# ODE stage of a four-layer hybrid network: sums left in PSUM, tanh read from there twice, the low part by a scan, 48 matmuls of four columns

## The reference

```
f(y) = tanh(tanh(y W1' + b1) W2' + b2) W3' + b3        (W1: 512x128, W2: 512x512, W3: 128x512)
k1 = f(y); k2 = f(y + dt/2 k1); k3 = f(y + dt/2 k2); k4 = f(y + dt k3)
y  = y + dt (k1 + 2 k2 + 2 k3 + k4) / 6
```

## Time and profile before

| what | value |
|---|---|
| median of 3 runs | 8713.31 us (8688.4 to 8720.65) |
| the profiled execution: its own time, its span | 8689.44 us, 8687.6 us |
| mean granted TensorE clock | 0.929 |
| PE matmul busy | 8034.5 us (92%) |
| PE weight loads busy | 5075.3 us (58%) |
| DVE busy | 5725.2 us (66%) |
| ACT busy | 2697.7 us (31%) |
| POOL busy | 1221.5 us (14%) |
| L803, the real matmuls of the products | 3940.5 us in 130816 |
| L815, `keep_busy` | 3260.8 us in 12264 |
| first and last matmul of the products start at | 899.9 and 7459.1 us |

### The profile page before, as it was taken

The page is one execution under the profiler, slowest core; times in us unless marked ns, Lnnn a source line. Parts: engine busy times, 40 slices in busy tenths (PEclk is TensorE's granted clock), DMA queues, the critical chain, the costliest instruction groups (busy, mean ns, idle before and its releaser), DMA issues. The chain is left out here.

```text
span 8687.6 us, 384742 instructions
## 1 busy us (share of the span) xinstructions
PE 8034.5 (92%) x148469; PEld 5075.3 (58%) x148469; DVE 5725.2 (66%) x32782; ACT 2697.7 (31%) x10082; POOL 1221.5 (14%) x5222
## 2 busy tenths in 40 slices
PE   8994899999999999999999999999999999765886
PEld 3221566666666666666666666666666666444765
DVE  4334666666666666666666666666666666546997
ACT  2221222222222222222222222222222222235886
POOL 1000111111111111111111111111111111001001
PEclk7665999999999999999999999999999999767887
DMA  1000000100010000100010001000000000002332
GB/s 43 1 0 32 15 4 4 38 4 4 4 38 4 4 4 4 38 4 4 4 38 4 4 4 38 4 4 4 8 34 4 4 4 20 3 0 109 121 126 75
DMA packets 44973, 185.48 MB, mean 21 GB/s; under 512 B 7156, under 2 KB 27319, under 8 KB 33031
## 3 DMA queue, kind: packets, MB, share of 16 engines
q1 hardware_dynamic: 38662, 145.18, 4.4%
q0 software_dynamic: 4480, 15.38, 0.5%
HBM read 122.93 MB, written 37.62 MB: 18 GB/s over the span
## 5 line engine op out<-in xcount | busy, mean ns | idle before, releaser
L803 PEld LDWEIGHTS p<-H,W 128*128 128x128 f16 x130816 | 3571.6, 96 | 1931.7 <-DVE H L954 1914.2
L803 PE MATMUL p<-H,W 128*128 128x8 f16 x130816 | 3940.5, 167 | 66.1 <-DVE H L954 59.1
L815 PE MATMUL p<-W 128*128 128x500 f16 x12264 | 3260.8, 374 | 0.0
L954 DVE SCALAR_TENSOR_TENSOR H<-h,H 128x8 f16<-128x8 f32 x10220 | 1505.7, 164 | 282.0 <-DVE H L949 2.6
L889 ACT ACTIVATE h<-u 128x8 f32<-128x8 f32 x4088 | 852.2, 208 | 2428.2 <-DVE u L980 2269.3
L884 ACT ACTIVATE h<-r 128x8 f32<-128x8 f32 x4088 | 851.6, 208 | 2404.6 <-DVE r L988 2217.7
L988 DVE TENSOR_REDUCE r<-p 128x8 f32<-128x24 f32 x4088 | 746.1, 183 | 1050.9 <-PE p L803 809.9
L980 DVE TENSOR_REDUCE u<-p 128x8 f32<-128x24 f32 x6132 | 964.9, 175 | 717.8 <-PE p L803 716.9
L949 DVE TENSOR_SCALAR H<-h 128x8 f16<-128x8 f32 x8176 | 1400.1, 171 | 40.8 <-ACT h L884 21.7
L815 PEld LDWEIGHTS p<-W 128*128 128x128 f16 x12264 | 886.0, 96 | 473.4 <-issue 9.3
L779 POOL TENSOR_TENSOR twice<-r 128x16 f32<-128x16 f32 x511 | 110.2, 216 | 2860.1 <-DVE r L988 2860.1
(11 more groups left out here) (364 smaller groups left out, 4211.5 us busy)
## 6 DMA issues: line engine op xcount, KB each, us to landing
e_W<-w_scaled SPq DMA_DIRECT2D x23, 2304.0 KB
e_W<-w_scaled SPq DMA_DIRECT2D x23, 1152.0 KB, 5.2
raw_f<-in_spline SPq DMA_DIRECT2D x21, 1024.0 KB, 6.3
w_scaled<-raw_f SPq DMA_DIRECT2D x7, 2304.0 KB, 7.6
w_scaled<-raw_f SPq DMA_DIRECT2D x7, 1152.0 KB, 11.2
raw<-in_spline POOLq DMA_DIRECT2D x3, 1024.0 KB, 6.8
rows_in<-zeros POOLq DMA_DIRECT2D x4, 768.0 KB, 12.5
e_xs<-rows_in SPq DMA_DIRECT2D x12, 256.0 KB, 5.6
```

The source lines that it names most:

```text
L803: ins = pe.matmul(out[:, m, 0:2 * B], W[:, q, k, P * m:P * m + P], H[:, k, :, :].rearrange("p q b -> p (q b)"), start=fresh[m], stop=(left ...
L815: pe.matmul(out[:, k, 3 * B:S], W2[:, 0, k, 0:P], W2[:, 1, k, 3 * B:S], start=True, stop=True, skip_group_check=True)
L954: sg.up(dve.scalar_tensor_tensor(out=Hq[:, :, 1, :], in0=mb(cols(h, q)), scalar=HSCALE, in1=Hq[:, :, 0, :], op0=ALU.mult, op1=ALU.subtract ...
```

## The change

- `keep_busy`, the scale of 4096 on H, the reductions (L980, L988), `high` and `low` go.
- The sums stay in PSUM. Every product adds on top of a seed that DVE writes into columns 0 to 3 of each bank beforehand (`start=False` everywhere; eight matmuls with zeros before the loop). The first product on `p2` is seeded with b2, by a copy of `b2s`; `p1` is seeded with the Runge-Kutta terms.
- ACT takes tanh straight from PSUM, twice: once into H (fp16) and once into h (fp32).
- The output chunks go in three groups, (0), (1, 2) and (3), in both layers: six ACT instructions to a product.
- H, h and L hold three slots for each value; constants in slots 1 and 2 make one DVE scan along the line leave 4096 (h - H) in slot 1 of L.
- The low part is multiplied by the high weight part alone, scaled down by 4096 (`W2D`, `W13D`). A block is then two matmuls with H and one with L: 48 matmuls of 4 columns, in the order of one list BLOCKS for both layers, where "h" stands for two matmuls and "l" for one.
- DVE copies `p1` into r once the tanh has been taken, and POOL works from that copy.

```
-    FILL = 3
-    RED2, LOW2 = [(0, 1), (2,), (3,)], [(0, 1), (2,), (3,)]
...
+    GROUPS = [(0,), (1, 2), (3,)]
+    G = len(GROUPS)
+    LIFT = 4096.0
+    BLOCKS = [("h", 0, 2), ("h", 0, 3), ("h", 0, 0), ("h", 0, 1), ("h", 2, 0), ("h", 2, 2), ("h", 2, 1), ("h", 1, 0), ("l", 0, 2),
+              ("h", 3, 1), ("h", 3, 2), ("l", 1, 2), ("l", 1, 0), ("l", 0, 0), ("l", 2, 1), ("l", 0, 3), ("l", 1, 1), ("l", 2, 0),
+              ("h", 3, 0), ("l", 3, 0), ("h", 1, 1), ("l", 3, 2), ("l", 2, 2), ("h", 1, 2), ("l", 3, 1), ("l", 0, 1), ("h", 3, 3),
+              ("l", 2, 3), ("h", 1, 3), ("l", 3, 3), ("l", 1, 3), ("h", 2, 3)]
...
+        H1, H2 = sb("H1", [P, NV, 3], F16), sb("H2", [P, NV, 3], F16)
+        h1, h2 = sb("h1", [P, NV, 3]), sb("h2", [P, 4, NV, 3])
+        L1, L2 = sb("L1", [P, NV, 3], F16), sb("L2", [P, NV, 3], F16)
...
+        def product(pe, i, w, e, out, W, WD, H, L, high, low, seeded, n_seeded, done):
+
+            wait(pe, seeded, n_seeded, w, i)
+            left, owed, high_in, low_in = [2 * KH] * KH, list(GROUPS), 0, 0
+            for part, k, m in BLOCKS:
+                group = next(n for n, q in enumerate(GROUPS) if k in q) + 1
+                if part == "h" and group > high_in:
+                    wait(pe, high, 2 * (G * e + group) - 1, w, i)
+                    high_in = group
+                if part == "l" and group > low_in:
+                    wait(pe, low, G * e + group, w, i)
+                    low_in = group
...
+                columns = slice(B * k, B * k + B)
+                terms = [(W[:, q, k, P * m:P * m + P], H[:, columns, 0]) for q in range(NP)] if part == "h" else [
+                    (WD[:, k, P * m:P * m + P], L[:, columns, 1])]
+                for n, (weights, x) in enumerate(terms):
+                    ins = pe.matmul(out[:, m, 0:B], weights, x, start=False, stop=(left[m] == 0 and n == len(terms) - 1), skip_group_check=True)
...
-        def keep_busy(pe, out):
-
-
-            for k in range(FILL):
-                pe.matmul(out[:, k, 3 * B:S], W2[:, 0, k, 0:P], W2[:, 1, k, 3 * B:S], start=True, stop=True, skip_group_check=True)
...
+                        product(pe, i, w, e, p2, W2, W2D, H1, L1, "h1", "lo1", "seed2", e + 1, "u2")
+                        product(pe, i, w, e, p1, W13, W13D, H2, L2, "h2", "lo2", "seed1", e + 1, "u1")
...
+            for n, (wd, whole) in enumerate(((W2D, W2), (W13D, W13))):
+                sg.wait(act, "part", n + 1)
+                sg.up(act.activation(wd[:], whole[:, 0], ACT.Copy, scale=1.0 / LIFT), "part")
...
+                            for n, q in enumerate(GROUPS):
+                                wait(act, "u1", G * e + n + 1, w, i)
+                                for x in (H1, h1):
+                                    sg.up(act.activation(mb(cols(x[:, :, 0], q)), sums(p1[:, q[0]:q[-1] + 1]), ACT.Tanh, scale=factor[c]), "h1")
...
+            def low(H, h, L, layer, e, n, w, i):
+                wait(dve, f"h{layer}", 2 * (G * e + n + 1), w, i)
+                sg.up(dve.tensor_tensor_scan(flat(cols(L, GROUPS[n])), flat(cols(H, GROUPS[n])), flat(cols(h, GROUPS[n])), -1.0, ALU.mult, ALU.add), f"lo{layer}")
...
+                        for n in range(G):
+                            low(H1, h1, L1, 1, e, n, w, i)
+                        before = r[:, (e + 3) % 4, :]
+                        sg.up(dve.tensor_copy(mb(before), sums(p1)), "copied")
+                        wait(dve, "copied", e + 1, w, i)
...
+                        for n in range(G):
+                            low(H2, h2[:, e], L2, 2, e, n, w, i)
+                        sg.up(dve.tensor_copy(sums(p2), mb(b2s[:])), "seed2")
```

More of the change, by code:

```diff
@@ L745, in flow @@
         mb = lambda x: x.rearrange("p (m b) -> p m b", b=B)
-        terms = lambda x, q: x[:, q[0]:q[-1] + 1, 0:3 * B].rearrange("p m (q b) -> p m b q", b=B)
-        seed = lambda x: x[:, :, 2 * B:3 * B]
+        flat = lambda x: x.rearrange("p n s -> p (n s)")
+        sums = lambda x: x[:, :, 0:B]
         splits = [(w2f[:], lambda q: W2[:, q]), (w13f[:], lambda q: W13[:, q])]
@@ L769, in _ @@
             sg.up(pool.memset(hist[:, :, STEPS:S, :], 0.0), "ones_set")
+            sg.up(pool.memset(zero[:], 0.0), "zeros")
+            for x in (H1, H2):
+                sg.up(pool.memset(x[:, :, 1], LIFT), "zeros")
+                sg.up(pool.memset(x[:, :, 2], 0.0), "zeros")
+            sg.up(pool.memset(h1[:, :, 1], 0.0), "zeros")
+            sg.up(pool.memset(h1[:, :, 2], -1.0), "zeros")
+            for e in range(4):
+                sg.up(pool.memset(h2[:, e, :, 1], 0.0), "zeros")
+                sg.up(pool.memset(h2[:, e, :, 2], -1.0), "zeros")
             sg.wait(pool, "ones_set", 3)
@@ L781, in _ @@
                     sg.up(pool.tensor_tensor(base[:], twice[:], third[:], ALU.add), "base")
[L783 to L786, removed]
+                    wait(pool, "h2", 6 * G, w, i)
+                    sg.seq(pool, pool.tensor_tensor(inner[:], h2[:, 1, :, 0], h2[:, 2, :, 0], ALU.add), "hsum", i)
+                    wait(pool, "h2", 8 * G, w, i)
+                    sg.seq(pool, pool.tensor_tensor(outer[:], h2[:, 0, :, 0], h2[:, 3, :, 0], ALU.add), "hsum", i)
                     sg.seq(pool, pool.tensor_tensor(both[:], inner[:], outer[:], ALU.add), "hsum", i)
@@ L837, in _ @@
             sg.wait(pe, "rest", 2)
+            sg.wait(pe, "zeros", 1)
+            for x in (p1, p2):
+                for m in range(KH):
+                    ins = pe.matmul(x[:, m, 0:B], W2[:, 0, m, 0:P], zero[:], start=True, stop=True)
+                sg.up(ins, "cleared")
             with pe.Fori(0, STEPS // UN) as i:
@@ L959, in _ @@
                     for e in range(4):
-                        at1, at2 = len(HIGH1) * e, len(HIGH2) * e
-                        high(h1, H1, 1, (0, 1), at1 + 1, w, i)
-                        low(h1, H1, 1, (0, 1), at1 + 1, w, i)
-                        high(h1, H1, 1, (2, 3), at1 + 2, w, i)
-                        low(h1, H1, 1, (2, 3), at1 + 2, w, i)
+                        for n in range(G):
[3 more added lines that the diff above has]
+                        wait(dve, "copied", e + 1, w, i)
+                        if e < 3:
+                            seed = dve.scalar_tensor_tensor(out=sums(p1), in0=mb(r[:, 3, :]), scalar=(1.0 / 3.0, 1.0 / 3.0, 1.0 / 6.0)[e], in1=mb(hb[:]), op0=ALU.mult, op1=ALU.add)
+                        else:
+                            wait(dve, "base", 6, w, i)
+                            seed = dve.scalar_tensor_tensor(out=sums(p1), in0=mb(r[:, 2, :]), scalar=2.0, in1=mb(base[:]), op0=ALU.mult, op1=ALU.add)
+                        sg.up(seed, "seed1")
                         if e == 1 and 4 <= w < 4 + 2 * ExpertWeights.PARTS:
```

99 lines of the change are left out of this document (24 added, 75 removed).

## The result

The changed kernel takes 8748.31 us (median of 20 runs, 8709.89 to 8759.08); the kernel before took 8712.25 beside it (20 runs, 8677.12 to 8734.51). The ratio is 1.0035, 95% interval 1.0022 to 1.0048. I had predicted 7485 in a range of 7270 to 8200, so the time lies outside the range: no gain, a small loss. It is rival C in mechanism, to which I had given 0.07 and a time of 8,620.

The account below looks back on a forecast made before the run. It took the round trip PE, DVE, ACT (1.583 us a product) as the bound, then PE's own work: 2216.9 us plus 4087 x 1.282 = 5239.5 gives a span of 7456, carried over to 7482, given as 7485; range 7270 to 8200.

Parts of the forecast that it names:

- rival C: PE in the ODE waits for its instruction packets; a product takes 1.4 to 1.56 us, up to 8,620 us; chance 0.07.
- the time table: One product step by step: every input reaches PE in time by 0.03 to 0.14 us, so PE's 1.282 us binds.
- The 1.07 us: Time an instruction packet itself takes in the DMA engines, held against waiting for instructions.
- the 3.7 us of the turn: PE's standstill at each of six loop turns, 22 us in all; also taken as a possible time per instruction packet.
- break-even: Product time in the ODE at which the change gains nothing: 1.583 us.
- The clock: PE without filler runs at 1.2 GHz (0.50) through the ODE, 3 in 4; 26.7 ns a pair, 1.282 us a product.
- D: PE can't keep its pace beyond a burst; slower than before from 33 ns a pair, at most 11,110 us; chance 0.11.
- ACT and DVE: Per product, six tanh of 183 ns, starting 0.11 us apart, and DVE scans of 185 and 210 ns.
- B: The round trip by ACT and DVE clearly binds each product; 7,720 to 8,300 us; chance 0.22.
- The rest of the sum: Outside the products: 899.9 + 3.7 ahead, 81 for turns and hiccups, 1229.3 + 3 behind; 2216.9 us.
- The two copies: Two more ACT copies of 1.91 us in set-up before the loop, adding 3.7 us.
- my formula: Whole kernel time T = 2242.6 + 4087 p, for a product of p us.

Follow-up runs that it names:

- pe_loop_7: Changed kernel with PE's loop rolled up to seven evaluations (14 products, some 1400 instructions) as its body: 7547.14 us, 0.8701 of the kernel before.
- low_twice_loop: Changed kernel with each of the 16 low-part matmuls of a product issued twice and PE looping over one evaluation: 9361.79 us.
- pe_loop_1: Changed kernel with PE's loop rolled up to one evaluation (2 products, some 200 instructions) as its body: 7753.09 us, 0.8923 of the kernel before.
- pe_loop_14: Changed kernel with PE's loop over 14 evaluations (28 products, some 2800 instructions) as its body: 9384.56 us.
- two_groups: Changed kernel, still unrolled, with output chunks in two groups, (0, 1) and (2, 3), instead of three, and BLOCKS to fit: 8469.70 us, 0.973 of the changed kernel.
- act_pool_loop: Changed kernel, PE unrolled, with only ACT's and POOL's loops rolled up to one Runge-Kutta step: 8683.04 us, 0.9984 of the kernel before.
- one_filler: Changed kernel with one unread matmul of 508 columns added to each product to raise the clock: 9328.39 us.
- no_low: Changed kernel with the 16 low-part matmuls of a product left out of PE's work, scans still running: 6837.18 us.

## Why the prediction was wrong

**The step that failed** is the conclusion of the time table, "So PE's own work becomes the bound", which took instructions to be always at hand, together with the weight of rival C: "packets themselves take 1.07 us [...], and PE's rows show next to no 'issue'. 0.07". What stood in its place: PE waited for its instructions, one packet in 4.10 us, so that a product took 1.616 us and not 1.282. The numbers of C were all there: 7.0 KB a product (measured 6.46), a packet used up in 3.0 us (the products at hand use one in 1.28 / 0.394 = 3.2), 3.7 us for a packet if it is as slow as at the turn (4.10). What I did wrong was to hold two rows against it that say nothing of it. The 1.07 us is what a packet's bytes take in the DMA engines; between two packets of PE's queue lie 3.8 to 4.1 us in the kernels kept waiting, while that queue fills 1.7 to 1.9% of the DMA engines. And the absence of "issue" in the kernel before only said that 5.6 us is enough. A rate that has never been asked for is not shown by a trace in which nobody waits for it. The nearest row was the 3.7 us of the turn, and it should have carried the sum; its own label names DVE, not "issue", which is why it can give C a price but no proof.

**C's size.** With 3.7 us it gave p = 1.56 and 8,620; measured are 4.10 and 8,748. There is a slip in it: 7.0 / 16.4 x 3.7 is 1.58 us, and 8,700, which is break-even. My range ended at 8,200, and I had counted C among the gains, while by its own numbers nothing was left to gain.

**The clock: right.** 0.50 through the ODE; between stalls and in pe_loop_7 a product takes 1.28 or 1.33 us where I had 1.282 from 26.7 ns a pair. That the pace of pairs holds beyond a burst (D) is shown by low_twice_loop.

**ACT and DVE: right.** Scans 183 and 208 ns for 185 and 210; tanh 181, 171 and 190 for 183; the distance of two tanh 0.07 for 0.11, better than I had. The row that I had read the 0.11 from the earlier trace rows gives 0.10, and the other one 0.08 by my 0.183. The round trip (B) didn't bind: the waits for ACT and DVE in the changed kernel are at most 28 of 1000 us, those of pe_loop_7 2.8. Why every second product takes 1.33 and not 1.28 I haven't found; the list BLOCKS is the same for both, so it isn't the list.

**The rest of the sum.** Ahead of the first product 7.8 us were added, not 3.7. The two copies take the 3.7 (they follow the last split of the weights from 902.47 and end ahead of the table load for tanh at 906.18); nearly all the rest lies ahead of that split, which starts at 900.66 instead of 896.03. The traces differ there anyway: the first product starts between 871.5 us (pe_loop_1) and 924.4 (pe_loop_14), and at 872.0 in two_groups, which is unrolled. Behind the last lie 8750.2 - 7518.5 = 1231.7 us; I had 1229.3 + 3. None of it matters. If I put the p of pe_loop_7 into my formula, 2242.6 + 4087 x 1.328 = 7,670, it lies 120 above the 7547 measured. The main reason is that a p counted over 1000 us has the turns and hiccups in it already, and the formula adds 81 us for them: for the kernel before, the p of 1.603 overshoots by 80 us in the same way. The first product of pe_loop_7 also starts 24 us earlier (879.3) than the formula has it, and its profiled execution lies only 2 below the median, not 24.

**So where did the gain go?** The chain through ACT and DVE did become short enough for PE's own work to be the bound, and the rolled-up kernels show what that is worth: 13% in pe_loop_7. In the unrolled one it went into PE's wait for instructions, 0.394 of a packet a product. The kernel before hid 0.29 of a packet (180 over 623.7 products) behind a chain of 1.58 us; the change took the cover away and asked for 37% more at once.

**The Trainium skill on this.** "Runtime: NRT & Kernel Launch", section "Instruction fetch mechanics", says that instructions come in blocks of 256, that PE holds 2048, that fetching them is hidden because issuing is slower than the fill, and that a taken branch outside a window of two blocks stalls. The runs agree on the block (64 bytes, 16.4 KB), and on the capacity as far as they go: 1400 stay, 2800 don't. They disagree with the fill being hidden (244 to 263 blocks in 1000 us, PE standing in between), and with the window of two blocks as a limit for loops: bodies of 800 and 1400 instructions turn without a fetch.

**What stays open.** What sets a packet's 3.80 us in one kernel and 4.10 in another. The other engines' packets don't (act_pool_loop), and the transfer of the expert weights, which does slow PE's queue, falls into the stretch of each of them. The changed kernel waits 28 us in 1000 for ACT and DVE, two_groups 6, and 22 us over 244 packets would be 0.09 of the 0.13 between them; but act_pool_loop waits 57 us for ACT and DVE at the same 4.08, so this is no explanation. Nor is it measured what the changed kernel would take at the full clock, since one_filler didn't raise it.

## What to carry to other kernels

Count the instructions of PE for each turn of the critical loop, and compare with 256 per 3.8 to 4.1 us, some 15 to 16 ns each here; where a loop of small matmuls is written out, that and not the spacing of weight loads (26.7 ns a pair, 13.4 an instruction) can be the limit, and it shows as idle time with "issue" at a place that moves. Then roll PE's program up into a body that stays (up to 1400 instructions here) and leave the other engines as they are; but not into one that doesn't stay (2800), which is worse than writing it out. And when a trace shows that a resource is not waited for, divide what it delivers by the time before taking it for free: what it delivered is a lower bound of what it can, and says nothing of more.

## What was not expected of the hardware

- PE's instructions come at 244 to 263 packets of 16.4 KB in 1000 us in the six kernels that wait mainly for them, 4.0 to 4.3 GB/s, with the DMA engines at 1.9% at most for it (no_low waits for them in part, with 228).
- While another queue moved 7.47 MB in 40 us (DMA share 0.49), 7 of these packets came in place of 10, and the changed kernel's PE ran 935 matmuls in place of 1202.
- A loop body of 1400 instructions turns without one packet from 930 to 6300 us, with 0.13 to 0.19 us for a turn; one of 2800 fetches 13 packets where 11 hold it.
- Two tanh of 4 columns out of PSUM start 0.07 us apart while each lasts 0.17 to 0.18.
- A matmul of 508 columns in every product of some 50 small ones left the clock at 0.50, and took 586 ns there.
